# Loading the opening tiles of the second half one at a time, with new places for its parts

## The chip, the core and the metric

The kernel runs on one core of a Trainium2 chip. The metric is the device time in microseconds (us), taken as the median of repeated runs. All data is float32; some products are done as three products of parts that were split beforehand (a high part and the rest).

## What is computed

A layer over x of shape (2, 1024, 2048), 2048 tokens in all, cut to what matters:

```python
h = layernorm(x)
q_in, k_in, v_in = rat_read(h, 3)             # per-channel mix of 4, then normalised, 512 wide
o = causal_attention(q_in, k_in, v_in)        # 16 heads of 32, rope
h = rat_write(h, o, wod1, wab1, du1)          # after attention
g, u = rat_read(h, 2)
y = silu(g @ W0.T) * (u @ W1.T)               # 2048 wide, W from ctx, per layer
h = rat_write(h, y, wod2, wab2, du2)          # after the MLP
x = x + h
x = x + 2 * experts(layernorm(x))             # 8 experts of rank 16, softmax router
```

`rat_write` projects its input to 512 outputs, 8 low values and 112 gate values; `delta = softplus(low @ du + b)`; `A = exp(delta * A_neg)`; and h, seen as 512 groups of 4, becomes `h * A + out * B`, elementwise over 2048 columns.

## The kernel before, in words

The tokens are 16 tiles of 128, and 4 blocks of 4 tiles. The program has three phases, and this case is about the third: `project_*` (q, k, v), `attend_*` (attention; beside it the MLP weights are split and stored), and `mix_*` (all the rest, the second half).

**Order.** In the second half each engine (TensorE, ACT, DVE, POOL, SP) walks one common list, `order` (lines 1359 to 1369), and does its own share of each entry, waiting on semaphores. The list is sorted by place: a number that is the tile's start (tables `a`, `w`, `e` of `PLACES`) plus the part's offset (tables `A` or, for the first four tiles, `FIRST`; `W`; `E`). One unit of place is one of the 64 m steps of a block: steps 0 to 31 are the MLP's first products (12 matmuls of 512 columns), 32 to 63 the second (`m_wods`, 12 of 316 columns). `t` places the turning of a block's y into `m_y_split`, `h` the splitting of the MLP's middle.

- `a`, the write after attention of tile i: `loado` loads its attention, `load` its x, `wod` is the product with the output weights (16 matmuls; ACT and DVE take the results), `low` and `delta` small products, `gates`, `scale`, `sum` the elementwise work, on DVE above all (`sum` is lines 1763 to 1772), four `turn`s and four `read`s of a quarter each (turning h and mixing it), `stats` and `norm`.
- `w`, the write after the MLP, and `e`, the experts: `turn`, `down`, `router`, `weigh`, `lowT`, four `out`s and `store`.
- `m` step 63 of a block ends its products; DVE and ACT then take the sums of its four tiles.

**Weights.** All weights of the second half go through five buffers (`NW`, line 327), in the order of use. At an entry `a.wod` SP issues four loads (line 1493), each after the product that freed its buffer. So tile 0's `wod` on SP issues the weights of quarters 1 to 3 of tile 1 and of quarter 0 of tile 2; the fifth buffer holds quarter 0 of tile 1 from before.

**Buffers that order the work.** The first four tiles have buffers of their own for x and attention (`hs_of`, `f_oT`), so their loads need wait for nothing. Turns, `low`, `delta`, `lowT` and `out` share a ring of PSUM banks (`one`, line 1417): four in the opening, banks 6 and 7 from block 0's y turns until the last step of the last block. A turned quarter goes to one of two buffers, free when the `read` or `down` of the quarter two before is done. The y turns of block 2 write buffers which block 1's second products still read, two per turn, the last pair until step 63.

**SP** issues every DMA, in list order: before a store it waits until the tile is ready (`turn` 0 of `a`: stores h after `sum`), and all that is behind it on SP waits too.

Of the kernel before, what the change touches and what calls it, by code (L numbers as in the profile page):

```python
# [53 lines left out]

PLACES = {'A': {'loado': -5.2,
       'wod': 0,
       'low': 2.8,
       'load': 4.08,  # L60
# [4 lines left out]
       'turn0': 13.72,  # L65
       'turn1': 14.22,
       'read0': 15.22,
       'turn2': 15.72,
       'read1': 16.41,
       'turn3': 16.72,  # L70
       'read2': 17.94,
       'read3': 17.95,
       'stats': 17.96,
       'norm': 18.88},
 'W': {'load': -0.23, 'low': 0, 'delta': 1.6, 'gates': 2.51, 'loadx': 3.49, 'scale': 4.46, 'sum': 5.28, 'x': 6.33},
 'E': {'mean': 8.68,
       'turn0': 9.86,
       'turn1': 10.81,
       'spread': 12.99,
       'down0': 13.81,  # L80
       'turn2': 14.0,
       'down1': 14.24,
       'turn3': 14.33,
       'down2': 15.58,
       'down3': 15.59,
       'router': 16.32,
       'weigh': 16.61,
       'lowT': 18.86,
       'out0': 20.28,
       'out1': 22.31,  # L90
       'out2': 23.3,
       'out3': 23.31,
       'store': 23.32},
 'FIRST': {'loado': -100.02,
           'load': -98.38,
           'wod': 1.52,
           'low': 2.23,
           'delta': 3.23,
           'gates': 3.24,
           'scale': 3.25,  # L100
           'sum': 5.74,
           'turn0': 7.26,
           'turn1': 7.27,
           'turn2': 7.75,
           'turn3': 7.76,
           'read0': 9.23,
           'read1': 9.24,
           'read2': 9.51,
           'read3': 10.01,
           'stats': 12.14,  # L110
           'norm': 13.63},
 'a': {0: -200,
       1: -197,
       2: -193.88,
       3: -191,
       4: -2.68,
       5: 10.52,
       6: 22,
       7: 34.81,
       8: 54.57,  # L120
       9: 66.44,
       10: 83.01,
       11: 94.12,
       12: 118.84,
       13: 132,
       14: 145.3,
       15: 159.5},
 'w': {0: 64,
       1: 76,
       2: 92.34,  # L130
       3: 103.69,
       4: 127.69,
       5: 140,
       6: 155,
       7: 166.75,
       8: 192,
       9: 204,
       10: 218.97,
# [2 lines left out]
       13: 243.3,  # L141
       14: 256,
       15: 258},
 'e': {0: 64,
       1: 76,
       2: 91,
       3: 103.14,
       4: 129.08,
       5: 142.08,
       6: 155,  # L150
       7: 170.99,
       8: 193.45,
       9: 205.58,
       10: 223.5,
       11: 234.51,
       12: 239.56,
# [1 line left out]
       14: 254.71,  # L158
       15: 260.44},
 't': [-1.77, -1.44, -1.12, -0.79, -0.46, -0.13, 0.2, 0.53, 55.15, 56.07, 57.0, 57.92, 58.85, 59.78, 60.7, 61.63,  # L160
       120.81, 121.9, 122.99, 124.07, 125.16, 126.25, 127.34, 128.43, 182.13, 183.53, 184.93, 186.33, 187.73, 189.13,
       190.53, 191.93],
 's': 30.5,
 'h': [30.22, 30.72, 30.94, 31.22, 31.44, 32.5, 32.72, 32.73, 33.64, 33.73, 34.44, 35.24, 35.89, 36.69, 37.49, 37.78]}


class Engine:
# [51 lines left out]
def program(nc, x, xT, pos, inv_freq, ident_in, causal_in, spread_in,  # L219
# [3 lines left out]
    with ExitStack() as ctx:  # L223
# [1122 lines left out]
        def prepare_dve():  # L1346
# [11 lines left out]

        placed = [(PLACES["s"], ("s", 0, "sum", None))]
        placed += [(64 * blk + step, ("m", blk, step, None)) for blk in range(NBLK) for step in range(64)]  # L1360
        placed += [(64 * blk + at, ("h", blk, "split", m)) for blk in range(NBLK) if SPLIT[blk]
                   for m, at in enumerate(PLACES["h"])]
        placed += [(at, ("t", n // 8, "turn", n % 8)) for n, at in enumerate(PLACES["t"])]
        for i in range(NT):
            for what, table, base in (("a", "FIRST" if i < TB else "A", "a"), ("w", "W", "w"), ("e", "E", "e")):
                for part, at in PLACES[table].items():
                    q = int(part[-1]) if part[-1].isdigit() else None
                    placed.append((PLACES[base][i] + at, (what, i, part.rstrip("0123"), q)))
        order = [entry for at, entry in sorted(placed, key=lambda p: p[0])]
# [871 lines left out]
```

How the kernel before makes its waits and increments, by code:

```python
    def wait_ge(self, sem, value):  # L173
        if value > self.met.get(sem.name, 0):
            self.met[sem.name] = value
            self.e.wait_ge(sem, value)
# [8 lines left out]
    def then_inc(self, instruction):  # L185
        self.n += 1
# [317 lines left out]
        def project_pe():  # L504
            pe.wait_ge(memsets_done, ONES1)
            flat = read1[:, :, :, :].rearrange("p a b c -> p (a b c)")
            for n in range(3):
                pe.wait_ge(tables_ready, n + 1)
# [4 lines left out]
            def read(i):  # L513
                b = read_bank(i)
                pe.wait_ge(xT_loaded[i % 2], 16 * (i // 2 + 1))
                if b:
                    pe.wait_ge(tables_ready, WSUM)
                pe.wait_ge(z_ready, i - 1 if i <= TB else i)
                for j in range(DCH):
                    m = nc.tensor.matmul(ps[:, b + j // 4, zw * (j % 4):zw * (j % 4) + zw], p_xT[i % 2][:, j, :],
                                         read1[:, j, :, :].rearrange("p a b -> p (a b)"), start=True, stop=True)
                m.then_inc(read1_mm, 1)
# [1 line left out]
            def turn(blk):  # L524
                pe.wait_ge(ident_loaded, 16)
                if blk == 0:
                    pe.wait_ge(z_ready, TB)
                def one_of(k, q):
                    o, hc = divmod(k, HCH)
                    b, i = 4 + k % 4, blk * TB + q
                    pe.wait_ge(y1_ready, RD1 * i + o + 1)
                    return nc.tensor.transpose(ps[:, b, P * q:P * q + P],
                                               p_y[i % YR][:, o, P * hc:P * hc + P], ident[:, :])
```

## Time and profile before

| | us |
|---|---|
| median of 3 runs | 1674.62 |
| lowest and highest | 1673.56, 1676.0 |
| the profiled execution | 1670.99 |
| its span, first to last instruction | 1669.2 |

| engine | busy us | share of the span |
|---|---|---|
| TensorE (PE) | 1545.9 | 93% |
| DVE | 1142.0 | 68% |
| ACT | 906.8 | 54% |
| GpSimd (POOL) | 337.0 | 20% |

The projection takes the first 300 us or so, attention runs until 617 us, the opening (tiles 0 to 3 after attention, before any MLP product) until about 717 us, blocks 0 to 3 until about 1604, and the experts of the last tiles end it. Shares are averages over these stages; what a change in one of them is worth is read from that stretch. In a timeline, the number in brackets is how long the engine was idle before, and what ended it; "issue" means nothing that the profile shows. PEclk is the clock granted to TensorE, as a part of 2.4 GHz. The rows come from the one profiled execution.

### The profile page before, as it was taken

What the parts mean: (1) busy time and instruction counts of PE and PEld (TensorE: products, weight loads), DVE (VectorE), ACT (ScalarE), POOL (GpSimd) and SP (SyncE); (2) the same over time, 40 slices, a digit from 0 to 9 for tenths busy, and PEclk for the clock granted to TensorE, in tenths of its full rate; (3) what the DMA queues carried; (4) which work ended last, traced back from release to release, by engine and by line L of the source; (5) the groups of instructions that cost most, each with busy time, mean ns of one, the idle gap of its engine ahead of it and who ended that gap; (6) DMA issues with size and microseconds to landing.
All of it is one profiled execution on the core that took longest, in us unless ns stands there. A gap on an engine that the chain in (4) does not pass through costs nothing.

```text
span 1669.2 us, 24979 instructions
## 1 busy us (share of the span) xinstructions
PE 1545.9 (93%) x9430; PEld 1159.3 (69%) x9430; DVE 1142.0 (68%) x1790; ACT 906.8 (54%) x1672; POOL 337.0 (20%) x327
## 2 busy tenths in 40 slices
PE   7999999999999985799999999799999999999976
PEld 6565555666666653678898777697778788875554
DVE  7877754888888866753473685874786864636776
ACT  5334235888888864555543656553557724552443
POOL 1434435555434500020002000012000002000001
PEclk8999999999999996799999999999999999999997
DMA  9658567999987735367677765567665656656632
GB/s 359 218 195 309 179 170 232 275 292 281 269 222 206 214 129 204 114 237 238 209 225 236 246 227 202 173 234 237 236 243 200 230 189 223 223 186 210 222 147 101
DMA packets 129624, 364.81 MB, mean 219 GB/s; under 512 B 15968, under 2 KB 45280, under 8 KB 114144
## 3 DMA queue, kind: packets, MB, share of 16 engines
q1 hardware_dynamic: 129216, 363.08, 67.1%
q8 instruction: 75, 1.23, 0.3%
q14 instruction: 45, 0.37, 0.1%
q10 hardware_dynamic: 288, 0.13, 0.0%
HBM read 277.04 MB, written 86.11 MB: 218 GB/s over the span
## 4 chain that ended last, share of the span: by engine, by line
PE 76%; DVE 13%; ACT 6%; issue 3%; DMA 2%; POOL 0%; SPq 0%; DVEq 0%; ACTq 0%
PE ps L1654 21%; PE ps L1666 8%; PE ps L561 7%; PE ps L1054 5%; PE ps L1041 4%; PE ps L1077 4%; PE ps L1566 4%; PE ps L1679 4%; PE ps L1597 3%; ACT a_p L1156 3%; PE ps L1551 3%; PE ps L1612 3%; PE ps L520 3%; PE ps L1624 2%; PE ps L533 1%
## 5 line engine op out<-in xcount | busy, mean ns | idle before, releaser
L1654 PE MATMUL ps<-m_y_split,m_win 128*128 128x512 f32 x1536 | 376.0, 398 | 2.9 <-issue 2.9
L1654 PEld LDWEIGHTS ps<-m_y_split,m_win 128*128 128x128 f32 x1536 | 285.1, 189 | 64.5 <-issue 7.5
L1098 DVE TENSOR_REDUCE a_negmax<-ps 128x1 f32<-128x640 f32 (+7 forms) x176 | 180.6, 1026 | 59.6 <-PE ps L1044 58.8
L1156 ACT ACTIVATE a_p<-ps,a_negmax 128x128 f32<-128x128 f32 (+7 forms) x256 | 188.6, 750 | 29.2 <-DVE a_negmax L1098 26.8
L1666 PE MATMUL ps<-m_wods,m_y_split 128*128 128x316 f32 x768 | 178.2, 321 | 3.0 <-DVE m_hT L1854 2.6
L1892 ACT ACTIVATE m_turned<-ps 128x512 f32<-128x512 f32 x128 | 75.1, 594 | 162.6 <-PE ps L1551 148.6
L1054 PE MATMUL ps<-ident,a_p 128*128 128x128 f32 x1152 | 157.6, 275 | 1.4 <-DVE a_pT L1111 1.2
L1041 PE MATMUL ps<-a_k,a_q 128*128 128x512 f32 (+3 forms) x384 | 123.9, 402 | 16.2 <-ACT a_p L1156 14.3
L1666 PEld LDWEIGHTS ps<-m_wods,m_y_split 128*128 128x128 f32 x768 | 127.7, 191 | 7.9 <-issue 3.9
L1054 PEld LDWEIGHTS ps<-ident,a_p 128*128 128x128 f32 x1152 | 123.7, 142 | 3.4 <-DVE a_pT L1111 1.9
L2039 POOL TENSOR_TENSOR m_scale<-m_scale,mhalf 128x2 f32<-128x2 f32 x16 | 12.0, 747 | 538.3 <-DVE m_scale L1790 538.3
L1666 PE MATMUL ps<-m_wods,m_hT_lo 128*128 128x316 f32 x384 | 118.4, 308 | 0.0
L561 PE MATMUL ps<-p_yT,p_wqkv 128*128 128x512 f32 x256 | 112.1, 593 | 0.0
L1210 POOL TENSOR_SCALAR a_w_two<-a_w_raw 128x512 fp32r<-128x512 f32 (+1 forms) x64 | 80.6, 1260 | 146.4 <-DMA mlp_in_split<-a_w_two 71.7
L1854 DVE TENSOR_TENSOR m_hT<-m_raw,ps 128x512 f32<-128x512 f32 x64 | 43.9, 686 | 96.8 <-PE ps L1654 96.3
L1111 DVE COPY a_pT<-ps 128x512 f32<-128x512 f32 (+3 forms) x190 | 107.8, 574 | 0.9 <-PE ps L1054 0.4
L1170 ACT ACTIVATE a_pT<-ps 128x512 f32<-128x512 f32 (+3 forms) x154 | 83.9, 546 | 33.6 <-PE ps L1054 33.4
L1041 PEld LDWEIGHTS ps<-a_k,a_q 128*128 128x128 f32 x384 | 63.2, 192 | 54.5 <-ACT a_p L1156 31.3
L1551 PE MATMUL ps<-ident,m_hs 128*128 128x128 f32 x464 | 73.1, 288 | 26.1 <-DVE m_hs L1772 14.2
L561 PEld LDWEIGHTS ps<-p_yT,p_wqkv 128*128 128x128 f32 x256 | 47.7, 190 | 55.5 <-issue 55.5
L1551 PEld LDWEIGHTS ps<-ident,m_hs 128*128 128x128 f32 x464 | 58.7, 150 | 36.7 <-DVE m_hs L1772 14.8
L1077 PE MATMUL ps<-a_pT,a_v 128*32 128x256 f32 (+3 forms) x1152 | 76.7, 385 | 0.7 <-ACT a_pT L1170 0.7
(219 smaller groups left out, 2925.9 us busy)
## 6 DMA issues: line engine op xcount, KB each, us to landing
m_win<-mlp_in_split SPq DMA_DIRECT2D x128, 512.0 KB, 4.3
m_wods<-mlp_out_split SPq DMA_DIRECT2D x96, 316.0 KB, 3.3
m_wod<-in_wod1T SPq DMA_DIRECT2D x64, 316.0 KB, 2.9
p_xT<-in_xT SPq DMA_DIRECT2D x16, 1024.0 KB, 9.1
p_x<-in_x SPq DMA_DIRECT2D x16, 1024.0 KB, 10.5
a_q<-qk_split SPq DMA_DIRECT2D x64, 256.0 KB, 7.1
a_k<-qk_split SPq DMA_DIRECT2D x128, 128.0 KB, 7.2
mlp_in_split<-a_w_two SPq DMA_DIRECT2D x32, 512.0 KB, 5.8
```

The source lines that it names most:

```text
L561: m = nc.tensor.matmul(ps[:, b, :], wq[:, k, col:col + P], yT[:, k, :], start=(ic == 0), stop=(ic == HCH - 1))
L1041: nc.tensor.matmul(ps[:, bank + at, c0:c0 + kn], qs[s][:, qt * P:qt * P + P], ks[s][:, k0:k0 + kn], start=True, stop=k0 + kn < klen)
L1054: m = nc.tensor.transpose(ps[:, b, P * m_:P * m_ + P], src[:, j, P * k:P * k + P], ident[:, :])
L1077: m = nc.tensor.matmul(ps[32 * hh:32 * hh + 32, 6, c0:P * qn], a_v[s][:, k, HD * hh:HD * hh + HD], kept[:, hh, k, c0:P * qn], start=(k == ...
L1098: V.tensor_reduce(negmax[:, n % 4, 0:len(units[n][3])], by_head(n, score_banks(n)), AX_X, ALU.max, negate=True).then_inc(max_ready, 1)
L1111: V.tensor_copy(kept[:, heads[j0]:heads[j1] + 1, k0:k1 + 1, P * q:P * q + P], ps[:, b, 0:P * len(part)].rearrange("p (a k b) -> p a k b", ...
L1156: m = S.activation(dst[:, j, :], src[:, j, :], ACT.Exp, bias=negmax[:, n % 4, j:j + 1], accum_out=rsum[:, si % 2, q * 4 + hh:q * 4 + hh + 1])
L1170: S.activation(kept[:, heads[j0]:heads[j1] + 1, k0:k1 + 1, P * q:P * q + P], ps[:, b, 0:P * len(part)].rearrange("p (a k b) -> p a k b", a ...
L1210: m = pool_own.then_inc(G.tensor_scalar(w_two[s][:, 0, 0:w], w_raw[r][:, 0:w], 1.0, None, ALU.mult))
L1551: m = nc.tensor.transpose(bank_of(what, i, "turn", q)[:, P * j:P * j + P], h[:, P * (4 * q + j):P * (4 * q + j) + P], ident[:, :])
L1654: m = nc.tensor.matmul(bank_of("m", blk, step), win[s][:, wl, ic, :], y[k], start=(ic == 0 and p3 == 0), stop=(ic == HCH - 1 and p3 == 2))
L1666: m = nc.tensor.matmul(bank_of("d", blk, q, r)[:, 0:HALFW], h[:, k, P * q:P * q + P], w2s[s][:, wl, :], start=(k == 0 and p3 == 0), stop=( ...
```

## The change

Only the table `PLACES` changes. The first four tiles' start values stay, but in `FIRST` the loads get offsets of -2 (attention) and -0.5 (x), where they had about -100 and stood ahead of all. With the tile starts (-200, -197, -193.88, -191) the list of the opening is now, for SP: x0, attention 1, `wod` 0, x1, attention 2, `wod` 1, x2, attention 3, `turn0` of tile 0 (its store), `wod` 2, x3, `wod` 3. Before it was x0, attention 1, x1, attention 2, x2, attention 3, x3, `wod` 0, `wod` 1, `turn0` of tile 0, `wod` 2, `turn0` of tile 1, `wod` 3.

On the other engines the opening changes in three spots. Tile 2's `wod` stands between `turn0` and `turn1` of tile 0 (before: behind `turn1`). Tile 3's `wod` stands ahead of `turn0` of tile 1 and of tile 0's `read3` (before: behind `turn1` of tile 1). `read3` of tiles 1 and 2 stands behind `turn0` of the next tile (before: ahead).

Later: block 1's second half has tile w2's `sum` on DVE ahead of the `low` of a11 and of e1's first two outputs (before: behind a11's `low` and e1's first output); block 2's y turns come about three steps earlier, and tile 12's `gates` comes behind step 63 of block 1; in block 2 the write of tile 7 comes about two steps later, with e6's `weigh` ahead of its `scale`. Other parts move by less than a step or two.

```diff
-PLACES = {'A': {'loado': -5.2,
+PLACES = {'A': {'loado': -6.07,
...
        'read0': 15.22,
+       'read1': 15.23,
        'turn2': 15.72,
-       'read1': 16.41,
-       'turn3': 16.72,
+       'turn3': 16.91,
...
- 'W': {'load': -0.23, 'low': 0, 'delta': 1.6, 'gates': 2.51, 'loadx': 3.49, 'scale': 4.46, 'sum': 5.28, 'x': 6.33},
+ 'W': {'load': -0.23, 'low': 0, 'delta': 1.26, 'gates': 2.51, 'loadx': 3.16, 'scale': 4.46, 'sum': 5.28, 'x': 6.48},
...
-       'down0': 13.81,
+       'down0': 13.1,
...
-       'router': 16.32,
+       'router': 15.93,
        'weigh': 16.61,
-       'lowT': 18.86,
-       'out0': 20.28,
-       'out1': 22.31,
-       'out2': 23.3,
-       'out3': 23.31,
-       'store': 23.32},
- 'FIRST': {'loado': -100.02,
-           'load': -98.38,
-           'wod': 1.52,
-           'low': 2.23,
-           'delta': 3.23,
-           'gates': 3.24,
-           'scale': 3.25,
-           'sum': 5.74,
-           'turn0': 7.26,
-           'turn1': 7.27,
-           'turn2': 7.75,
-           'turn3': 7.76,
-           'read0': 9.23,
-           'read1': 9.24,
-           'read2': 9.51,
-           'read3': 10.01,
-           'stats': 12.14,
-           'norm': 13.63},
+       'lowT': 18.72,
+       'out0': 20.14,
+       'out1': 22.17,
+       'out2': 23.16,
+       'out3': 23.51,
+       'store': 23.87},
+ 'FIRST': {'loado': -2,
+           'load': -0.5,
+           'wod': 1.37,
+           'low': 2.86,
+           'delta': 3.86,
+           'gates': 3.87,
+           'scale': 3.88,
+           'sum': 6.38,
+           'turn0': 7.41,
+           'turn1': 7.91,
+           'turn2': 8.39,
+           'turn3': 8.4,
+           'read0': 9.76,
+           'read1': 9.87,
+           'read2': 10.15,
+           'read3': 10.65,
+           'stats': 12.77,
+           'norm': 14.26},
...
-       12: 118.84,
+       12: 119.31,
...
-       7: 166.75,
+       7: 168.94,
...
- 'e': {0: 64,
-       1: 76,
-       2: 91,
+ 'e': {0: 62.89,
+       1: 77.98,
+       2: 91.84,
...
-       120.81, 121.9, 122.99, 124.07, 125.16, 126.25, 127.34, 128.43, 182.13, 183.53, 184.93, 186.33, 187.73, 189.13,
+       117.8, 118.94, 120.08, 121.22, 122.36, 123.5, 124.64, 125.79, 182.13, 183.53, 184.93, 186.33, 187.73, 189.13,
...
- 'h': [30.22, 30.72, 30.94, 31.22, 31.44, 32.5, 32.72, 32.73, 33.64, 33.73, 34.44, 35.24, 35.89, 36.69, 37.49, 37.78]}
+ 'h': [30.11, 30.61, 30.83, 31.11, 31.33, 32.39, 33.22, 33.59, 34.13, 34.22, 34.93, 35.63, 35.73, 35.83, 35.92,
+       36.39]}
```

## Rows read from the trace of the kernel before

**Rows 1.** Windows: stretch, its length, busy per engine, PEclk, DMA share, GB/s

```profile
630.00:635.00 5.00, 0.00 (x0) 0.00 (x0) 3.07 (x5) 1.35 (x1) 0.00 (x0) 0.50 1.00 405
...
720.00:1600.00 880.00, 847.66 (x4756) 692.28 (x4755) 545.92 (x780) 453.38 (x710) 64.21 (x66) 0.99 0.65 218
...
1060.00:1080.00 20.00, 12.75 (x75) 10.92 (x74) 16.57 (x18) 9.50 (x19) 0.00 (x0) 0.83 0.20 65
```

**Rows 2.** Timeline, opening of the second half: start, duration, engine [idle <- releaser]

```profile
617.92 4.56 PE L1566 MATMUL ps<-m_wod,m_oT 128*128 128x512 f32 x16 [0.59 <-issue]
...
619.92 0.33 SPq L259 DMA_DIRECT2D m_hs<-in_x  x1
...
623.49 4.05 SPq L259 DMA_DIRECT2D m_wod<-in_wod1T  x5
...
625.55 1.63 PE L1566 MATMUL ps<-m_wod,m_first_oT 128*128 128x512 f32 x4 [0.73 <-DMA m_first_oT<-attention_out]
...
632.15 1.06 DVE L1760 TENSOR_TENSOR m_hs<-m_hs,m_tmp 128x512 f32<-128x512 f32 x1
...
635.13 5.94 PE L1566 MATMUL ps<-m_wod,m_first_oT 128*128 128x512 f32 x12 [7.96 <-DMA m_wod<-in_wod1T]
...
641.11 0.28 DVE L1716 TENSOR_TENSOR m_mlp_ab<-ps,m_gate_bias 128x120 f32<-128x120 f32 x1 [7.90 <-PE ps L1566]
...
642.59 1.76 DVE L1763 TENSOR_TENSOR m_hs<-m_hs,m_A 128x1536 f32<-128x1536 f32 x1
```

**Rows 3.** DMA issues, 619.8 to 624: us from issue to landing is last

```profile
m_hs<-in_x SPq DMA_DIRECT2D x1, 1024.0 KB, 4.9
...
m_first_oT<-attention_out SPq DMA_DIRECT2D x1, 256.0 KB, 5.2
...
m_first_hs<-in_x SPq DMA_DIRECT2D x1, 1024.0 KB, 11.3
...
m_wod<-in_wod1T SPq DMA_DIRECT2D x1, 316.0 KB, 11.6
```

**Rows 4.** Timeline, second to fourth tile of the opening

```profile
649.66 1.97 PE L1551 MATMUL ps<-ident,m_hs 128*128 128x128 f32 x8 [6.55 <-DVE m_hs L1772]
...
651.42 5.64 PE L1566 MATMUL ps<-m_wod,m_first_oT 128*128 128x512 f32 x16
...
656.89 1.04 PE L1551 MATMUL ps<-ident,m_hs 128*128 128x128 f32 x8
...
657.10 0.28 DVE L1716 TENSOR_TENSOR m_mlp_ab<-ps,m_gate_bias 128x120 f32<-128x120 f32 x1 [1.57 <-PE ps L1566]
...
670.85 1.11 DVE L1760 TENSOR_TENSOR m_hs<-m_hs,m_first_tmp 128x512 f32<-128x512 f32 x1
...
673.84 0.28 DVE L1716 TENSOR_TENSOR m_mlp_ab<-ps,m_gate_bias 128x120 f32<-128x120 f32 x1 [1.88 <-PE ps L1566]
...
675.10 0.29 DVE L1723 CAST m_first_lowT<-ps 128x128 fp32r<-128x128 f32 x1 [0.98 <-PE ps L1577]
```

**Rows 5.** Timeline, end of the opening

```profile
691.91 7.06 PE L1597 MATMUL ps<-m_read,m_turned 128*128 128x64 f32 x32 [5.42 <-ACT m_y L1939]
...
695.88 1.76 DVE L1772 TENSOR_TENSOR m_first_hs<-m_first_hs,m_first_A 128x1536 f32<-128x1536 f32 x1
...
698.76 3.27 PE L1551 MATMUL ps<-ident,m_first_hs 128*128 128x128 f32 x16
```

**Rows 6.** Timeline, waits in blocks 1 and 2

```profile
1068.41 1.28 DVE L1868 TENSOR_TENSOR m_hT_lo<-m_hT,m_y_split 128x512 fp32r<-128x512 f32 x2
...
1069.73 0.69 DVE L1829 TENSOR_TENSOR m_hs<-ps,m_hs 128x512 f32<-128x512 f32 x1
...
1070.47 1.11 PE L1551 MATMUL ps<-ident,m_hs 128*128 128x128 f32 x4 [7.25 <-DVE m_hs L1829]
...
1164.20 0.43 PE L1577 MATMUL ps<-ident,m_mlp_ab 128*32 128x128 f32 x8 [2.83 <-ACT m_mlp_out L2008]
...
1347.32 0.47 PE L1619 MATMUL ps<-ident,e_weighted 128*128 128x128 f32 x1 [3.73 <-DVE e_weighted L1822]
```

More of the change, by code:

```diff
@@ L116 @@
        4: -2.68,
-       5: 10.52,
+       5: 10.13,
        6: 22,
@@ L122 @@
        10: 83.01,
-       11: 94.12,
-       12: 118.84,
+       11: 94.61,
+       12: 119.31,
        13: 132,
@@ L129 @@
        1: 76,
-       2: 92.34,
+       2: 92.04,
        3: 103.69,
-       4: 127.69,
+       4: 127.02,
        5: 140,
        6: 155,
-       7: 166.75,
+       7: 168.94,
        8: 192,
@@ L152 @@
        8: 193.45,
-       9: 205.58,
+       9: 205.11,
        10: 223.5,
```

## The prediction

> **What bounds the kernel now.** I read the sum of the windows first. From 720 to 1600 us TensorE is busy for 847.66 of 880.00 us [rows 1]; all that better places can take out of that stretch is the other 32.3 us, and a little where the granted clock is under 1.00. The opening of the second half, 617 to 711 us, is another matter: in 630 to 635 us TensorE runs nothing, the granted clock reads 0.50 (1.2 GHz, after the engine had been idle), and the DMA engines are at a share of 1.00 with 405 GB/s [rows 1]. So here a transfer ends last. The timeline says which [rows 2]: SP issues the first x tile at 619.92, then the other three with their attention, and only at 623.49 the output weights of tile 1. The issue list gives the landings [rows 3]: the first x takes 4.9 us, the first attention 5.2, the fourth x 11.3, and the first of those weights 11.6, so it lands at 623.49 + 11.6 = 635.09. TensorE starts tile 1's other twelve products at 635.13 after 7.96 us of DMA wait. Four x tiles of 1 MB and three attentions of 0.25 MB stand in front of 316 KB that are wanted at once.
>
> Behind this the opening is a chain of DVE and TensorE. DVE has tile 0's `scale` done at 633.21 and can't begin tile 1 before 641.11 (7.90 us idle); tile 0's `sum` (four passes of 1.76 us) waits behind tile 1's `wod` and `low` in DVE's order [rows 2]. Then one tile follows the other: `sum` ends, TensorE turns half a tile (8 transposes, 1.97 us), does the next tile's 16 products (5.64 us), then DVE takes them after 1.57 us idle. For the tile after that DVE idles 1.88 us ahead of `wod` and 0.98 us ahead of `low` [rows 4].
>
> **Part 1: loads one tile at a time.** The order on SP becomes: x0, attention 1, four weights (each once one of tile 0's four quarters of products is done), x1, attention 2, four weights, x2, attention 3, store of tile 0, four weights, x3. Nothing is added or taken away. Tile 0's products run from 617.92 for 4.56 us, a quarter each 1.14 us [rows 2], so the four weights can go out from about 620.7 to 622.5. In front of the first three stand only x0 and attention 1, which land at 624.8 and 625.5 [rows 3]. The landings of x0 and x3 (624.8 and 634.3) are 3.75 MB apart, 0.40 MB per us, so each weight needs 0.8 us: they land near 626.3, 627.1 and 627.9. The first quarter of tile 1's products ends near 627.2 (625.55 and 1.63), and twelve more take 5.94 us at the slow clock [rows 2], so 633.1 at the latest. That is level with DVE's 633.21. DVE then starts tile 1 at 633.25 and not 641.11: **-7.9 us**. DVE is next late, no longer the transfer. If the weights landed up to 3 us later than this the gain would be 5.
>
> What the moved loads now wait behind: x1 (2.5 us of data behind the fourth weight) lands near 631.5, and ACT scales it only when tile 1 has its `low` and `delta`, so after 633.3. x2 goes out near 633, x3 behind tile 2's products (near 648); each is needed one tile of some 16 us (641.11 to 657.10 [rows 2, 4]) after the one before. A load takes 4.9 us alone and 11.3 in the crowd [rows 3], so the DVE work of a tile hides it. The weights of the next tile wait for the same products as before. Store 0 keeps its place after `sum`; SP is held there, but what is behind it is needed one tile later. I cost all this at nothing; without the cover of DVE it would cost at most those 4.9 us once.
>
> **Part 2: the FIRST places.** On TensorE tile 2's products now follow the first quarter turn of tile 0, and the other three turns come behind them. The products end 1.0 us earlier (half of 1.97), but `low` comes after 12 transposes and not 8, at 0.13 us each (1.04 for 8) [rows 4], 0.5 us back: **-0.4 us**. The Trainium skill's "TensorE: Matmul & The Clock Gate", Part 4, says that transposes don't count as busy time for the full clock. By it those 12 would cost 2.9 us and not 1.6, and this term would be +0.9. The row with 1.04 us for 8 stands right behind 16 products and is at the full rate; I go by it.
>
> Tile 3's products go ahead of tile 1's first turn, that is ahead of the wait for `sum`. They then run while DVE is in that `sum` (7.0 us, against 4.6 to 5.6 us of products and an idle TensorE); their weights were asked for one tile earlier. DVE has tile 2's `scale` done at 671.96 (670.85 and 1.11) and may start tile 3's `wod` at once, then waits for `low` only: 1.88 + 0.98 = 2.86 us idle before [rows 4], some 0.5 after (the path of `low` through TensorE, 0.98 at most). **-2.3 us**; bounds 0 (products late) and -2.9.
>
> In the end the last quarter of tile 2's reads (8 of 32 matmuls that took 7.06 us at the slow clock) comes behind tile 3's first turn. DVE's last `sum` ends at 697.64 (695.88 and 1.76) and TensorE begins the turns at 698.76, since it still reads [rows 5]. Now they start at once, but the 1.76 us of reads lie between the first turn and the rest: **+0.6 us**. Behind it tile 4's products and block 0 follow as before.
>
> The opening: -7.9 - 0.4 - 2.3 + 0.6 = **-10.0 us**, bounds -5 and -12.
>
> **Part 3: new places later.** Block 0 keeps nearly all of its order, and its waits are small: nothing. Three waits of TensorE stand where the change moves something [rows 6]. (a) At 1070.47, 7.25 us: a turn needs one of the two banks, which DVE empties only behind a `sum` of 7.0 us and two splits (1.28) [rows 6]. Now `low`, the add of an output quarter (0.69) and one split (0.64) go behind that `sum` in DVE's order, so it starts about 1.9 us earlier, but they also stand ahead of the banks: -1.9, bounds 0 and -7.25. (b) At 1164.20, 2.83 us: the first `low` of block 2 waits since DVE does tile 12's `gates`, with a pass as long as one of `sum`'s, before it takes block 1's sums. `gates` moves behind them. But ACT now has the last of block 2's y turns ahead of its copies: -1.6 of the 2.83, bounds 0 and -2.83. The rest of the turns of y go some three steps earlier and wait on ACT for buffers that block 1's products still read; with the last one's bank free only at the end of block 1 they finish no later than before. (c) At 1347.32, 3.73 us: the expert's `lowT` waits for a weighing that stands behind a tile's `scale` on DVE (two passes like the one of 0.69 us [rows 6] and one of 1.06 [rows 2]); it moves ahead of it: -2.4. But then a turn needs the bank of an output quarter that DVE drains behind a `sum`: +1.5 to +2. The three sum to -1.9 - 1.6 - 2.4 + 1.8 = -4.1, taken as **-4 us**, bounds -14 (all three waits gone) and +4 (one new wait half of (a)'s, 3.6).
>
> **The sum.** The profiled execution is 1670.99 us with a span of 1669.2; -10.0 and -4.0 make 1656.99 and a span of 1655.2. The median is 3.63 above that execution, so 1674.62 - 14.0 = **1660.6 us**.
>
> **Rivals.**
> The opening gains only its DMA wait, and the second half gives nothing. For it: places that go ahead on TensorE don't help where DVE is full, and (a) and (c) each get back a similar wait. Against it: the 2.86 us of idle DVE are plainly there. 1674.62 - 7.9 = 1666.7.
>
> The second half gains nearly all of its three waits. For it: after each the clock is below 1.00 for a while (0.83 in 1060 to 1080 is 3.4 us more) [rows 1]. Against: the same DVE work must fit in. With 11 of those 14 us, 1674.62 - 10.0 - 11 = 1653.6.
>
> Slower: the two banks. In the middle of a block all turns, lows and output quarters go through two banks; the change puts a `sum` of 7 us ahead of a `low` and an output quarter in block 1 and ahead of an output quarter in block 2. If TensorE arrives at both with nothing else to do, each is a full wait of 7.25 us and 3.4 us for the clock, 10.65 us, on top of (a). 1674.62 - 10.0 + 21.3 = 1685.9. It decides as soon as new waits exceed 10.0 us, one such place. Against it: in both places the banks' drain moves by no more than the 2 us worked out above.
>
> The change doesn't do what it says: SP is in order, and if its waits for the products' quarters hold x1 back so long that ACT waits for it, the DMA wait is only renamed. x1 would have to land some 8 us later than worked out. Then the -7.9 is gone and, with nothing from part 3, 1674.62 - 2.1 = 1672.5 is left, inside what counts as no change.
>
> **How the numbers follow.** Forecast 0.67 (opening -8.5 to -11.5, later -8 to +1); opening only 0.16; all waits gone 0.10; slower 0.04; no effect 0.03. The forecast's own range is 1656 to 1666. With the first rival at 1666.7 taken in, and the other three (0.17 together) left out, it is 1655.5 to 1667.5. What a measurement of this kernel can tell from no change is about 0.2%, 3.3 us. Faster by more 0.93, within 0.03, slower 0.04.
>
> **What would show it.** After: tile 1's first weights land near 626, no DMA wait of 8 us is left, DVE's `wod` of tile 1 stands near 633.3; tile 3's products begin before tile 1's turn, DVE's idle time ahead of its third `wod` is nil, and block 0 begins ten us earlier. The waits (a), (b) and (c) stand near 5, 1 and 3 us. The prediction is wrong if DVE waits for tile 1's products beyond 636, if ACT waits for an x tile, or if a new wait over 4 us stands before a turn in block 1 or 2.

## The result, and the profile after

| | before | after |
|---|---|---|
| median, us | 1674.3 | 1650.24 |
| lowest and highest, us | 1673.56, 1676.0 | 1649.84, 1652.79 |
| the profiled execution, us | 1670.99 | 1652.79 |
| its span, us | 1669.2 | 1651.0 |
| TensorE busy, us | 1545.9 | 1548.6 |
| DVE busy, us | 1142.0 | 1138.4 |

The change makes the kernel 24.1 us faster: ratio 0.9854, 95% interval 0.984 to 0.9869. Forecast were 14.0 us and 1660.6; 1650.24 lies below the low end of 1655.5. The direction was right, the size was not. TensorE does the same work in less idle time. (The profiled execution of after is the slowest of its four. Its span is 18.2 us shorter than before's, which is a part of the 24.1. The section on the steps says where it lost some of it.)

Line numbers of after are one higher than before's. First the timeline of its opening, which answers to [rows 2]:

```profile
620.24 0.33 SPq L260 DMA_DIRECT2D m_hs<-in_x  x1
620.61 0.43 SPq L260 DMA_DIRECT2D m_first_oT<-attention_out  x1
621.09 2.16 SPq L260 DMA_DIRECT2D m_wod<-in_wod1T  x4
...
625.85 4.58 PE L1567 MATMUL ps<-m_wod,m_first_oT 128*128 128x512 f32 x16 [0.72 <-DMA m_first_oT<-attention_out]
...
632.46 1.06 DVE L1761 TENSOR_TENSOR m_hs<-m_hs,m_tmp 128x512 f32<-128x512 f32 x1
...
633.55 0.28 DVE L1717 TENSOR_TENSOR m_mlp_ab<-ps,m_gate_bias 128x120 f32<-128x120 f32 x1
```

The four weights go out at 621.09 and not 623.49. Tile 1's 16 products run in one piece of 4.58 us, where before four of them took 1.63 us and twelve waited 7.96 us for a transfer. DVE begins tile 1 at 633.55, forecast 633.25, right behind its work for tile 0: the transfer is no longer what ends last.

The second and third tile of the opening, to be read against [rows 4]:

```profile
640.29 1.76 DVE L1773 TENSOR_TENSOR m_hs<-m_hs,m_A 128x1536 f32<-128x1536 f32 x1
...
643.01 6.93 PE L1567 MATMUL ps<-m_wod,m_first_oT 128*128 128x512 f32 x16
649.78 1.47 PE L1552 MATMUL ps<-ident,m_hs 128*128 128x128 f32 x12
649.98 0.28 DVE L1717 TENSOR_TENSOR m_mlp_ab<-ps,m_gate_bias 128x120 f32<-128x120 f32 x1 [2.03 <-PE ps L1567]
...
654.49 4.54 PE L1567 MATMUL ps<-m_wod,m_first_oT 128*128 128x512 f32 x16
...
665.27 0.28 DVE L1717 TENSOR_TENSOR m_mlp_ab<-ps,m_gate_bias 128x120 f32<-128x120 f32 x1
...
666.33 0.29 DVE L1724 CAST m_first_lowT<-ps 128x128 fp32r<-128x128 f32 x1 [0.78 <-PE ps L1578]
```

Tile 3's products (654.49) now run beside tile 1's `sum`, so DVE starts tile 3 at 665.27 with no wait. Tile 2's products pay for the earlier place: 6.93 us where they took 5.64, and DVE waits 2.03 us for them and not 1.57.

Then the three waits of TensorE of [rows 6]. After has two rows in their place:

```profile
1060.21 1.11 PE L1552 MATMUL ps<-ident,m_hs 128*128 128x128 f32 x4 [3.82 <-DVE m_lowT L1726]
...
1152.88 0.42 PE L1578 MATMUL ps<-ident,m_mlp_ab 128*32 128x128 f32 x8 [0.94 <-ACT m_mlp_out L2009]
```

(a) went from 7.25 to 3.82 us, (b) from 2.83 to 0.94, and (c) is gone: the largest wait in block 2 is now 1.2 us. Forecast were about 5, 1 and 3.

### The profile page after: what moved, and what is told of

It reads as the page before. It is cut to its first block, busy times and chain, and to the rows that moved or that the text cites. A ratio compares the mean times of both kernels' runs of the same rounds, so it can differ in the third digit from the quotient of the medians.

```text
span 1651.0 us, 24981 instructions
## 1 busy us (share of the span) xinstructions
PE 1548.6 (94%) x9430; PEld 1162.4 (70%) x9430; DVE 1138.4 (69%) x1790; ACT 906.3 (55%) x1672; POOL 338.8 (21%) x327
## 4 chain that ended last, share of the span: by engine, by line
PE 75%; DVE 14%; ACT 7%; issue 3%; DMA 1%; POOL 1%; SPq 0%; DVEq 0%; ACTq 0%
PE ps L1655 21%; PE ps L1667 8%; PE ps L562 7%; PE ps L1055 5%; PE ps L1042 4%; PE ps L1078 4%; PE ps L1680 4%; PE ps L1567 3%; ACT a_p L1157 3%; PE ps L1613 3%; PE ps L1552 3%; PE ps L1625 3%; PE ps L1598 3%; PE ps L521 2%; DMA p_x<-in_x 1%
## 5 line engine op out<-in xcount | busy, mean ns | idle before, releaser
L1655 PEld LDWEIGHTS ps<-m_y_split,m_win 128*128 128x128 f32 x1536 | 284.6, 189 | 63.9 <-issue 7.0
L562 PEld LDWEIGHTS ps<-p_yT,p_wqkv 128*128 128x128 f32 x256 | 47.7, 190 | 55.5 <-issue 55.5
L2046 POOL TENSOR_SCALAR e_moments<-e_moments 128x1 f32<-128x1 f32 x16 | 11.5, 720 | 331.9 <-ACT m_x L1960 304.1
## 6 DMA issues: line engine op xcount, KB each, us to landing
p_x<-in_x SPq DMA_DIRECT2D x16, 1024.0 KB, 10.6
```

Source lines behind the costliest of these rows:

```text
L562: m = nc.tensor.matmul(ps[:, b, :], wq[:, k, col:col + P], yT[:, k, :], start=(ic == 0), stop=(ic == HCH - 1))
L1655: m = nc.tensor.matmul(bank_of("m", blk, step), win[s][:, wl, ic, :], y[k], start=(ic == 0 and p3 == 0), stop=(ic == HCH - 1 and p3 == 2))
```

## The experiments

All kernels differ from before or after in `PLACES` alone and compute the whole layer. "Tables" are the part offsets in `A`, `W`, `E` and the list `h`; "starts" are the values in `a`, `w`, `e`. To see where time goes I cut each trace at TensorE's first product of each half block. A half block then has a length, an idle time of TensorE (length minus busy) and a granted clock. Comparisons of lengths across kernels are between single profiled executions; of what such a difference is worth the medians decide. Before's profiled execution, 1670.99 us, is also 4 to 5 us faster than the medians of before beside the experiments (1674.76 to 1676.13), so differences of spans against it tend to come out too small. A gain "by the ratio" is one minus the ratio, times the median of before beside it.

### The opening and the rest, one at a time

e1_loads moves the loads alone, e2_first takes the whole of the new `FIRST`, e3_later everything but `FIRST`, and e4_block1_end only what the prediction tied to (b).

```diff
# e1_loads
- 'FIRST': {'loado': -100.02, 'load': -98.38,
+ 'FIRST': {'loado': -2, 'load': -0.5,
# e4_block1_end
-       12: 118.84,
+       12: 119.31,
...
-       120.81, 121.9, 122.99, 124.07, 125.16, 126.25, 127.34, 128.43,
+       117.8, 118.94, 120.08, 121.22, 122.36, 123.5, 124.64, 125.79,
```

> The kernel before with only the two load offsets of the opening changed (attention -2, x -0.5); all other places as before. Theory A (the transfer was the late thing, and DVE is next): the DMA wait of 7.96 us goes, tile 1's products end before DVE is free at 633.2, all later tiles keep their periods of 16.4 and 16.7 us, so -7.9 us at the last sum of the opening and -5 to -8 us in the total. Theory B (the slow clock of TensorE gives it back): the last sum of the opening comes 7 to 8 us earlier, but block 0 starts only 2 to 4 us earlier, since the y turns and tile 4's products run at 1.2 GHz; total -2 to -4 us.

> The kernel before with the whole table FIRST of the change, loads and places, and nothing else. As predicted: -10.0 us. After the trace of the changed kernel, where block 0 ends only 0.3 us earlier in the profiled execution, theory B: no better than the loads alone, -2 to -6 us, with tile 2's products slower (6.9 us against 5.6) and the reads of tiles 2 and 3 at 1.2 GHz. If it is 2 us or more better than the loads alone, the places of tile 3's products pay as predicted.

> The changed kernel with the old table FIRST: all later places, none of the opening. As predicted: -4 us. After the traces: block 1 8.7 us shorter, between blocks 1 and 2 2.4 us, block 2 6.3 us, tail 2.1 us, block 3 1.6 us longer, so -17 to -19 us in the total. The two parts add up to the change's -24 if they don't touch each other; a sum that misses it by more than 3 us says that they do.

> The kernel before with only block 2's y turns moved three steps earlier and tile 12's start moved from 118.84 to 119.31 (its gates then stand behind step 63 of block 1). The predicted mechanism (b): the wait of 2.83 us before the first low of block 2 falls to about 1.2 and the clock stays up, -2 to -4 us. Rival: block 2 begins sooner, but ACT, held by the early y turns, delays tile 12, and DVE gives the time back in block 2: 0 to -1 us.

| | median, us | before beside it | ratio | 95% |
|---|---|---|---|---|
| e1_loads | 1667.28 | 1675.18 | 0.9952 | 0.9937 to 0.9968 |
| e2_first | 1666.06 | 1675.18 | 0.9942 | 0.992 to 0.9963 |
| e3_later | 1657.76 | 1675.18 | 0.989 | 0.9869 to 0.9912 |
| e4_block1_end | 1668.42 | 1675.18 | 0.9967 | 0.9945 to 0.9989 |

The loads alone give 7.9 us, the whole opening 9.1, the later places 17.4. 9.1 and 17.4 are 26.5; the whole change gave 24.1, so the two add up to within what the intervals allow. What was missing from the forecast is in the later places, forecast -4. e4 with its one wait is worth 5.5 us by the ratio (6.8 by the medians, 3.3 by the spans of the profiled executions); the interval reaches from 1.8 to 9.2 us.

Where e3_later gains its 16.7 us of span, cut as above (length in us, idle TensorE in us). 0.7 us of it lies ahead of block 0; the stretches left out differ by 0.1 us at most:

| | before | e3_later |
|---|---|---|
| block 0 | 195.3, 1.6 | 197.2, 1.3 |
| block 1, first half | 135.0, 2.2 | 131.2, 1.0 |
| block 1, second half | 109.7, 10.5 | 104.8, 4.5 |
| between blocks 1 and 2 | 4.0, 2.8 | 1.6, 0.9 |
| block 2, first half | 136.3, 3.4 | 133.1, 2.4 |
| block 2, second half | 95.4, 5.5 | 92.3, 3.1 |
| block 3, second half | 97.4, 2.8 | 98.9, 2.6 |
| tail | 66.1, 23.2 | 63.9, 21.2 |

The window of block 1's second half holds (a); before and e3_later, columns as in [rows 1]:

```profile
1050.90:1160.60 109.70, 99.25 (x669) 88.51 (x668) 72.68 (x109) 48.38 (x87) 13.05 (x12) 0.97 0.62 203
```

```profile
1048.40:1153.20 104.80, 100.29 (x678) 90.03 (x677) 71.13 (x108) 48.43 (x89) 14.98 (x13) 0.97 0.65 216
```

The same work on every engine within 2 us, and 4.9 us less time. Two of the gains are in places to which the prediction gave nothing, block 1's first half (3.8 us) and the tail (2.2 us).

### Tables, starts, and the one start of tile 7

```diff
# e5_tables (A, W, E, h; of these, for instance)
-       'router': 16.32,
+       'router': 15.93,
-       'out0': 20.28,
-       'out1': 22.31,
+       'out0': 20.14,
+       'out1': 22.17,
# e6_bases (all the starts but a[12]; of these, for instance)
-       2: 92.34,
+       2: 92.04,
-       11: 94.12,
+       11: 94.61,
# e7_w7
-       7: 166.75,
+       7: 168.94,
# e8_wod3 (on e1_loads)
-           'wod': 1.52,
+           'wod': 1.2,
```

> The kernel before with only the offset tables A, W, E and h of the change (where the parts of a tile stand within the tile, and the splits of the MLP's middle); tile starts, y turns and FIRST as before. Theory O (the offsets do it: in the middle of block 1 the sums of tile w2 start earlier and the experts' outputs come later, so DVE reaches the two banks sooner): block 1's second half loses 4 to 6 us of its 10.4 us of idle TensorE, the total is -7 to -10. Theory S (the tile starts do it, the offsets only shuffle): total 0 to -3.

> The kernel before with only the tile starts a, w and e of the change (without tile 12's), offsets and y turns as before. Theory S: block 1's first half -1 and second -5, block 2 -3 to -6, total -7 to -12. Theory O: total 0 to -5, almost all of it block 2, where tile w7 starts two steps later.

> The kernel before with tile w7's start moved from 166.75 to 168.94 and nothing else: mechanism (c) alone. As predicted: the wait of 3.73 us before e6's lowT in block 2 falls to about 1.3, with 1.5 to 2 us given back at a bank drained behind w7's sum, in total -0.6. Rival: the wait goes whole and nothing comes back, and the clock stays at full rate behind it, so block 2's second half is 3 to 5 us shorter.

> The loads moved as in e1_loads, and of FIRST's other places only the wod offset, 1.52 to 1.2, which puts tile 3's products ahead of tile 1's turns and leaves tile 2's products and all reads where they were. If my term of -2.3 us holds and the rest of FIRST's places is what gives it back: 2 us better than the loads alone, so 1665 against 1667.3. If DVE's gain is lost at the end of the opening whatever the places (TensorE at 1.2 GHz for the last reads and tile 4's products): within 1 us of the loads alone.

| | median, us | before beside it | ratio | 95% |
|---|---|---|---|---|
| e5_tables | 1674.94 | 1676.13 | 0.9992 | 0.9983 to 1.0002 |
| e6_bases | 1671.11 | 1676.13 | 0.9968 | 0.9958 to 0.9978 |
| e7_w7 | 1671.36 | 1676.13 | 0.9971 | 0.9959 to 0.9983 |
| e8_wod3 | 1669.34 | 1676.13 | 0.9955 | 0.9939 to 0.9972 |

e7 settles (c). One start, that of tile 7's write, is worth 4.9 us by the ratio. Block 2's second half, before and e7:

```profile
1300.90:1396.30 95.40, 89.92 (x635) 84.16 (x633) 62.16 (x93) 44.11 (x79) 10.96 (x12) 0.98 0.57 184
```

```profile
1300.80:1393.30 92.50, 89.08 (x635) 83.10 (x634) 62.05 (x93) 44.11 (x79) 11.76 (x12) 1.00 0.58 190
```

2.9 us shorter: 2.1 of it is idle time (5.48 to 3.42) and 0.84 is work that runs faster, as the granted clock goes from 0.98 to 1.00. The new wait of 1.5 to 2 us that the prediction set against it isn't there; the longest wait in that half is 1.31 us. The interval of e7's 4.9 us is 2.8 to 6.9, so the 2.9 us of the profile fit it.

e5 and e6 don't give (a). The half block with (a) goes from 109.7 us to 108.3 with the tables (-1.4), and to 112.0 with the starts (+2.3). TensorE's idle time in it falls in both, from 10.5 to 8.6 and to 9.0 us; e6's is longer all the same because its matrix work took 103.0 us and not 99.3, at a granted clock of 0.94 and not 0.97. e5's rows show the wait only smaller, e6's that another took its place:

```profile
1072.94 1.12 PE L1551 MATMUL ps<-ident,m_hs 128*128 128x128 f32 x4 [5.78 <-DVE m_hs L1829]
```

```profile
1066.71 1.11 PE L1551 MATMUL ps<-ident,m_hs 128*128 128x128 f32 x4 [5.52 <-DVE m_lowT L1725]
```

The tables also lose 4.1 us in block 2's second half (95.4 to 99.5), where wait (c) is 6.16 us in e5 and was 3.73 in before. That eats what they gain elsewhere: e5 as a whole can't be told from before.

e8 puts tile 3's products where after has them and leaves the rest of `FIRST` alone. DVE's way from tile 0's `wod` to the end of tile 3's `sum` gets hardly shorter (66.1 us in e1, 65.7 in e8), and the time not at all. With the later places in force the same step takes it from 67.5 us (e12, below) to 64.1 (e9), and the time is again the same.

### Both together, and the tables with the start of tile 7

e10_tables_bases is the tables and the starts, with a[12], `t` and `FIRST` as before; e11_tables_w7 is the tables and w[7]. e9_after_wod3 and e12_after_loads are after, with the `FIRST` of e8 and of e1.

```diff
# e12_after_loads, against after: all of FIRST but the loads is put back
-           'wod': 1.37,
-           'low': 2.86,
+           'wod': 1.52,
+           'low': 2.23,
...
-           'sum': 6.38,
-           'turn0': 7.41,
+           'sum': 5.74,
+           'turn0': 7.26,
```

> The later places without the y turns of block 2 and without tile 12's start: offset tables and the other tile starts together (e5_tables and e6_bases in one kernel). If the parts add up: 1676.1 - 1.3 - 5.4, so -7 us. If offsets and starts need each other, as e3_later says (-17 to -18 for all, against -1.3 - 5.4 - 5.5 for its three parts): -11 to -13, with block 1's second half near 104 us (109.7 before, 108.3 and 112.0 alone) and block 2's near 92 (95.4 before, 99.5 and 92.5 alone).

> The offset tables of e5_tables with tile w7's start of e7_w7. If the loss of 4 us that the tables alone bring in block 2's second half (99.5 against 95.4) is the wait (c) grown longer, w7's start cures it: block 2's second half 92 to 93, total -8 to -10. If it is something else in the tables, block 2 stays near 96 and the total is -5 to -6 (the sum).

> The changed kernel with FIRST as in e8_wod3 (the two loads moved, wod at 1.2, all else of FIRST old). If FIRST's places are worth nothing but the loads and tile 3's products: the same as the changed kernel within 1.5 us, 1649 to 1651. If they matter as I predicted (-2.7 for the two places of products, +0.6 for the reads): 1 us faster than the changed kernel.

> The changed kernel with only the two loads of FIRST moved and the rest of FIRST old. By e1_loads and e2_first (1667.3 and 1666.1) FIRST's other places are worth 1 us: 1650 to 1652. If the places are needed with the later ones in force: over 1653.

| | median, us | before beside it | ratio | 95% |
|---|---|---|---|---|
| e10_tables_bases | 1663.25 | 1674.76 | 0.9928 | 0.9913 to 0.9942 |
| e11_tables_w7 | 1667.14 | 1674.76 | 0.995 | 0.9935 to 0.9965 |
| e9_after_wod3 | 1650.1 | 1674.76 | 0.9849 | 0.9834 to 0.9865 |
| e12_after_loads | 1649.8 | 1674.76 | 0.9852 | 0.9835 to 0.9868 |

The effects of tables and starts don't add: alone they give 1.3 and 5.4 us, together 12.1 (9.7 to 14.6). Tables and w[7] alone give 1.3 and 4.9, together 8.4 (5.9 to 10.9); there the times can't be told from the sum, but the profiles can, in one half block: the second of block 2 is 99.5 us with the tables, 92.5 with w[7], and 92.2 with both. The start of tile 7 also takes away what the tables lose there, the longer wait (c). Its windows, e5_tables and e11_tables_w7:

```profile
1302.90:1402.40 99.50, 90.61 (x635) 84.35 (x634) 62.81 (x93) 43.99 (x79) 11.36 (x12) 0.97 0.53 178
```

```profile
1302.70:1394.90 92.20, 89.11 (x635) 82.91 (x633) 62.84 (x93) 43.97 (x79) 11.04 (x12) 1.00 0.59 191
```

The first pair holds (a), in block 1's second half: -1.4 and +2.3 apart, -5.1 together (104.6 us); in idle time of TensorE -1.9 and -1.5 apart, -5.8 together. e10's timeline:

```profile
1043.12 4.48 PE L1566 MATMUL ps<-m_wod,m_oT 128*128 128x512 f32 x16
...
1055.87 1.76 DVE L1763 TENSOR_TENSOR m_hs<-m_hs,m_A 128x1536 f32<-128x1536 f32 x1
...
1063.48 1.11 PE L1551 MATMUL ps<-ident,m_hs 128*128 128x128 f32 x4 [3.82 <-DVE m_lowT L1725]
```

From the start of tile 11's products on TensorE to the start of tile w2's `sum` on DVE it is 12.75 us (1043.12 to 1055.87). In before it is 18.88: the products start at 1042.60, the `sum` at 1061.48. In e5 it is 18.45, in e6 13.97.

e9, e12 and after are the same within 0.5 us (1650.1, 1649.8, 1650.24). So the new places of `FIRST` other than the loads are worth nothing that can be measured in the whole kernel either (the intervals are some 2.5 us to either side).

### Is it only the place of w2's sum?

If only the time at which w2's `sum` starts counted, its start value alone should do it. e13_w2 moves it by 0.94 of a step; e14_tables_e12 adds the change's e[1], e[2] and w[2] to the tables; e15_after_w2 is after with w[2] a little earlier still.

```diff
# e13_w2, against before
-       2: 92.34,
+       2: 91.40,
# e14_tables_e12, against e5_tables
-       1: 76,
-       2: 91,
+       1: 77.98,
+       2: 91.84,
...
-       2: 92.34,
+       2: 92.04,
# e15_after_w2, against after
-       2: 92.04,
+       2: 91.40,
```

> The kernel before with tile w2's start moved from 92.34 to 91.40 and nothing else: its gates then stand ahead of a11's wod in DVE's order, and its scale and sum come ahead of e1's first output, three splits and a11's low. Theory P (what counts is how soon after TensorE's start of a11's products DVE begins w2's sum: 18.9 us before, 18.5 with the tables, 14.0 with the starts, 12.8 with both): here 12 to 14 us, the wait of 7.25 us falls to 1 to 4, block 1's second half from 109.7 to 104 to 106, total -4 to -6. Rival Q (the gain of 5 us needs the experts' outputs and the splits moved too): w2's place alone gives 0 to -2, the wait only moves to another bank.

> The offset tables, the starts of e1, e2 and w2 of the change; all other starts (a11 at 94.12 above all) as before. w2's gates then still stand behind a11's wod on DVE, while the experts' outputs and the splits are as in the change. Theory P: w2's sum begins 16 to 18.5 us after TensorE's start of a11's products and the wait stays 5 to 6 us, block 1's second half 107 to 109. Rival Q: wait near 3.8 us, second half near 105, as with all starts.

> The changed kernel with tile w2's start moved on from 92.04 to 91.40. Theory P: w2's sum begins 2 to 3 us sooner against TensorE, the remaining wait of 3.82 us falls to about 1, total 2 to 3 us below the changed kernel (1647 to 1648). Rival: DVE is full there in any case, and the wait comes back at the next bank: 1650.

| | median, us | before beside it | ratio | 95% |
|---|---|---|---|---|
| e13_w2 | 1672.75 | 1676.03 | 0.9979 | 0.9969 to 0.9988 |
| e14_tables_e12 | 1672.5 (one run) | 1676.03 | | |
| e15_after_w2 | 1652.36 | 1676.03 | 0.986 | 0.9844 to 0.9877 |

That simple form fell. In e13 the `sum` starts 13.93 us behind the products (1043.75 to 1057.68), 4.95 us sooner than in before, and yet the half block is 109.2 us long, 0.5 less. Three waits took the place of one:

```profile
1057.21 0.43 PE L1577 MATMUL ps<-ident,m_att_ab 128*32 128x128 f32 x8 [2.00 <-DVE m_hs L1829]
...
1066.47 1.12 PE L1624 MATMUL ps<-e_B,e_lowT 128*128 128x512 f32 x2 [2.33 <-DVE m_lowT L1725]
...
1070.72 1.12 PE L1551 MATMUL ps<-ident,m_hs 128*128 128x128 f32 x4 [2.90 <-DVE m_hs L1829]
```

Together 7.23 us. All idle time of TensorE in that half block does fall, from 10.5 to 8.0 us, but its work takes 2.0 us longer (99.25 to 101.22 us, granted clock 0.97 to 0.95). By the time, e13 gains 3.5 us (2.0 to 5.2), which lies between theory P and rival Q and doesn't decide between them. The wait of 7.25 us is 2.90, as P said, but the half block, which P put at 104 to 106 us, is far from it, also without the 2.0 us of slower work. e15 has its `sum` 12.1 us behind the products, as early as after, and waits 3.59 and 2.53 us; its half block is 108.0 us long, after's 104.7. It gains nothing over after, where 2 to 3 us were expected: 2.1 us slower by the medians, 1.0 by the ratios, whose intervals overlap. So the early `sum` isn't enough; that the order of the users of the two banks has to fit as well is my reading of where the waits moved, not shown by a run of its own. e14 doesn't reach it either (16.2 us behind the products, a wait of 5.17 for the bank, half block 108.8 us); it needs more of the starts that e10 has. Which of them, by itself, was not tried.

## Why the prediction was right and wrong

**What bounds the opening, and part 1.** Right. Forecast -7.9, measured 7.9 by the medians of e1_loads (8.0 by the ratio, 5.4 to 10.6). DVE was next late as said, and no x tile was waited for.

**Part 2.** Mechanisms right at their places, worth nothing in the sum. Tile 3's products were to bring -2.3 us: from the end of one `sum` to the next the third stretch went from 16.7 to 14.7 us, and DVE's idle ahead of `wod` to nil. But tile 2's term of -0.4 had the wrong sign. From `sum` to `sum` the second stretch went from 16.4 to 17.3 us, +0.9. I had counted the products at the 5.64 us of [rows 4]. Their first part runs at 1.2 GHz: TensorE had idled before (6.25 us in after), and after's granted clock is 0.50 from 644 to 646 us and 1.00 only from 648 on. In before eight transposes stood first and took a part of that slow time, in after only four, and the products are 6.93 us. How much of the 1.3 us is the order can't be said from this pair: with eight transposes first the same products took 5.07 to 6.35 us in the profiles of 14 kernels, with four first 6.47, 6.50 and 6.93 in three. At the end DVE's way from first `wod` to last `sum` is 65.7 us in after, 66.1 with the loads alone and 74.8 in before. So of -2.1 for part 2 there are -0.4 at DVE (-1.8 against the 67.5 of e12), and by the times of e12 and after nothing at the end. The twelve transposes behind those products took 1.47 us (649.78), so at the full rate. The Trainium skill's "TensorE: Matmul & The Clock Gate", Part 4, says that transposes don't count as busy time for the clock; the trace shows no more than that the clock stays up through twelve of them behind products.

**"Block 0 begins ten us earlier."** After's own profile shows only 2.2 (717.5 to 715.3). Its last reads of the opening and tile 4's products ran at the slow clock:

```profile
694.14 7.06 PE L1598 MATMUL ps<-m_read,m_turned 128*128 128x64 f32 x32
...
701.00 7.00 PE L1567 MATMUL ps<-m_wod,m_oT 128*128 128x512 f32 x16
```

The same two took 3.82 and 4.54 us in before and in e12_after_loads (694.64 and 698.30), 5.70 us less, and 4.34 and 4.54 in e2_first, whose `FIRST` is after's own. So the new places don't cause it. In e1, e2, e9 and e12 the first MLP product stands at 709.7 to 710.2, 7.3 to 7.8 us earlier than in before. Counted from DVE's first `wod`, which leaves out what came ahead of the opening, it is 8.7, 8.1, 10.0 and 7.0 us. After's median, equal to that of e9 and e12, suggests that its other executions don't show the loss; that is inferred, as only one of them is profiled. The opening: forecast -10.0, measured 8.0 (e1) and 9.7 us (e2) by the ratios.

**Part 3, the part that failed.** It was forecast at -4 and measured at -17.4 us. All three terms were too small: (a) -1.9 where the half block is 4.9 us shorter, (b) -1.6 where e4 gains 5.5, (c) -2.4 + 1.8 where e7 gains 4.9, and the tail, 2.2 us shorter, had no term.

**(a): the step with the wrong mechanism.** The step said that `low`, an output's add and a split go behind w2's `sum`, "so it starts about 1.9 us earlier". It starts 6.1 us earlier against TensorE (18.88 to 12.75). What I left out is what stands ahead of a *wait*. In before DVE meets tile 11's `wod` first and idles 1.51 us for TensorE's products; w2's `gates`, with a pass of 1.76 us and its small operations, stand behind it:

```profile
1047.19 0.28 DVE L1716 TENSOR_TENSOR m_att_ab<-ps,m_gate_bias 128x120 f32<-128x120 f32 x1 [1.51 <-PE ps L1566]
...
1050.38 1.76 DVE L1737 TENSOR_TENSOR m_A<-m_delta,m_gate 128x1536 f32<-128x1536 f32 x1
...
1061.48 1.76 DVE L1763 TENSOR_TENSOR m_hs<-m_hs,m_A 128x1536 f32<-128x1536 f32 x1
```

In after they are done before it:

```profile
1042.37 1.76 DVE L1738 TENSOR_TENSOR m_A<-m_delta,m_gate 128x1536 f32<-128x1536 f32 x1
...
1046.33 0.28 DVE L1717 TENSOR_TENSOR m_att_ab<-ps,m_gate_bias 128x120 f32<-128x120 f32 x1
...
1052.60 1.77 DVE L1764 TENSOR_TENSOR m_hs<-m_hs,m_A 128x1536 f32<-128x1536 f32 x1
```

The work that once stood behind the wait now fills it: from `wod` to `sum` it is 6.3 us (1046.33 to 1052.60), in before 14.3 (1047.19 to 1061.48). The row at 1042.37 is of w2. The half block is 4.9 us shorter in e3_later and 5.1 in e10, where the term was -1.9. e5 and e6 show that neither tables nor starts do it, e13 that an early `sum` alone doesn't. What the runs show, then, is how the `sum` comes early; why only tables and starts together turn that into time stays open in its last part.

**(b).** Forecast -1.6 of 2.83; the wait is 0.94, so the step holds. Its worth in time was mis-sized: in e4 the stretch between the blocks goes from 4.0 to 1.6 us, -2.4, and e4 gains 5.5 us of time, of which its profile places 2.4 here and 2.5 in block 2's first half, with +1.3 in block 1's second half. Block 2's first half is behind the stall. Its idle time falls too (3.4 to 2.7), and its first twelve products take 3.0 us where they took 4.49 in before, at the slow clock; but in e11 and e13, where the wait of 2.8 us stands, they take 3.0 as well, so the faster clock isn't the removed wait's for certain.

**(c).** Forecast -2.4 with 1.8 given back; measured 4.9 for w[7] alone. The wait goes and nothing is given back: the bank of the output quarter is free in time. 0.84 us of the 2.9 in its half block is the faster clock behind the vanished stall.

**Nothing for block 1's first half and for the tail.** The tail is wrong; the first half looks so, and is mostly the clock. The first half is 3.8 us shorter in e3_later, 1.2 of it idle time; the other 2.6 is the same work done faster, 1.6 of it behind a gap. Both kernels have the same gap ahead of block 1's products:

```profile
915.92 4.57 PE L1654 MATMUL ps<-m_y_split,m_win 128*128 128x512 f32 x12 [2.86 <-issue]
```

```profile
917.18 2.98 PE L1654 MATMUL ps<-m_y_split,m_win 128*128 128x512 f32 x12 [2.85 <-issue]
```

In before the granted clock then reads 0.50 and twelve products take 4.57 us, in e3_later it stays at 1.00 and they take 2.98. The windows behind it:

```profile
918.00:920.00 2.00, 2.00 (x6) 1.58 (x5) 1.15 (x1) 1.84 (x2) 0.00 (x0) 0.50 0.16 66
```

```profile
919.00:921.00 2.00, 2.00 (x16) 1.26 (x15) 1.16 (x2) 2.00 (x2) 0.00 (x0) 1.00 0.10 41
```

The gap is no shorter, so this 1.6 us was not won by any place I can name. Block 0 has the other side of it: its first twelve products take 2.0 us longer in e3_later, which is the 1.9 us that it is longer there.

```profile
717.50 3.02 PE L1654 MATMUL ps<-m_y_split,m_win 128*128 128x512 f32 x12
```

```profile
716.81 5.02 PE L1654 MATMUL ps<-m_y_split,m_win 128*128 128x512 f32 x12
```

The two go together in all 17 profiles. In six (after, e3, e5, e8, e11, e12) the products at the start of block 0 take 4.57 to 5.03 us and those at the start of block 1 2.98 to 3.00; in the other eleven it is 2.98 to 4.01 and then 4.53 to 4.59. So this is a slow stretch that falls in one place or the other, with about nothing in the sum. The 1.5 us that block 3's second half is longer are no idle time either (2.8 to 2.6): its work takes 96.3 us and not 94.7.

The tail gains 2.2 us. It comes with the tables (63.8 us in e5 against 66.1), not with the starts (66.5 in e6). The first wait for a weighing, 9.35 us in before and 7.14 in e3_later, is not its cause: it is 8.86 in e5 and 7.68 in e6. Which entry of the tables does it was not tried.

**The rivals.** "Opening only" is dead by e3_later, "no effect" and "slower" too. "All three waits gone" was the nearest (1653.6) and is also too slow. It counted only the waits: e3_later has 14.9 us less idle TensorE from block 0 on (55.5 to 40.7), of which the three waits explain 7.25 - 3.82, 2.83 - 0.94 and 3.73, together 9.1. The range failed there: its lower end took the waits as all there is.

No kernel tried beats after by more than can be measured.

## What to carry to other kernels

In an opening, ask which transfer ends last and put the small one that is wanted at once ahead of the large ones that are wanted later; here the price of the wrong order was its whole wait, 7.9 us, and the DVE work behind it was the next bound at once. When places of in-order engines change, don't cost only the instructions next to the stall: list every instruction that passes a point where that engine waits for another, because work moved ahead of such a wait fills time that was idle; here the `sum` behind it began 5 to 6 us earlier. Then look at what the early result meets: in e13 it met three other waits. And don't judge the parts of such a change one by one: here two sets of places gave 1.3 and 5.4 us alone and 12.1 together, and the start of one tile took away what the first set loses in one half block. Before a difference between two profiles is put down to a place, compare the granted clock in the same rows.

## What the runs showed of the hardware

A gap of TensorE of 2.85 us ahead of block 1's products was followed by half the clock in eleven of the 17 profiles (twelve products in 4.53 to 4.59 us) and by the full clock in six (2.98 to 3.00), and which of the two it was went with the clock at the start of block 0, some 200 us earlier. The last reads and products of the opening took 4.34 and 4.54 us in e2_first, and 7.06 and 7.00 in after, which has the same places there. A difference of 1.5 to 5 us in one stretch between two profiled executions can therefore be the clock alone.
